# Two steps of the feed-forward weights' preparation, moved from the first full pass of a software pipeline into the second

## The reference, cut to what matters

```python
x = x + layernorm(attn(layernorm(x)))          # rotary on half of each head, softmax, Wo
# feed-forward, on xn = layernorm(x)
base   = xn @ W.T
proj   = l2norm(xn @ Wp.T + bp)                # 32 wide
logits = proj @ l2norm(sim) * exp(min(temp, CLAMP_MAX))
lw     = softmax(logits)                        # 4 experts, of ranks 1, 2, 4, 8
ret    = lw where the expert is the top one, else 0
res    = sum over experts of ret[e] * (xn @ Wd[e].T) @ Wu[e].T
x = x + layernorm(base + res)
```

## Time and profile before

| | us |
|---|---|
| median of 3 runs | 167.34 |
| the three runs | 165.85, 167.34, 168.54 |
| the profiled execution, own time | 168.68 |
| its span, first to last instruction | 166.9 |
| its mean granted TensorE clock | 0.92 |

### The profile page before, as it was taken

How to read it: one execution, slowest core, us unless ns; L and a number is a source line. 1 busy time by engine, 2 the same in 40 slices (tenths; PEclk the granted TensorE clock), 3 DMA queues, 4 the chain that set the end, 5 groups by cost and what they waited for, 6 DMA issues and landing times.

```text
span 166.9 us, 3027 instructions
## 1 busy us (share of the span) xinstructions
PE 132.7 (80%) x865; PEld 108.6 (65%) x865; DVE 131.6 (79%) x560; ACT 112.0 (67%) x369; POOL 90.6 (54%) x150
## 2 busy tenths in 40 slices
PE   0468589967998999999999999999999799256030
PEld 0246267855887869887977897797889589145020
DVE  4669947586888899899979998897898889774512
ACT  3167535955979699879969996997998667240130
POOL 6272850670465586849657774976469516405202
PEclk9999957999999999999999999999999999965555
DMA  4533240000000000100010010001001000101001
GB/s 106 174 83 108 68 121 0 6 0 0 2 0 4 2 0 0 67 0 0 2 67 2 0 41 22 4 0 63 2 6 63 0 4 13 50 0 63 2 0 63
DMA packets 4912, 5.02 MB, mean 30 GB/s; under 512 B 369, under 2 KB 4640, under 8 KB 4896
## 3 DMA queue, kind: packets, MB, share of 16 engines
q1 hardware_dynamic: 4512, 4.46, 8.5%
q10 hardware_dynamic: 384, 0.38, 1.0%
HBM read 2.74 MB, written 2.10 MB: 29 GB/s over the span
## 4 chain that ended last, share of the span: by engine, by line
PE 46%; DVE 23%; ACT 18%; POOL 4%; DMA 3%; issue 3%; POOLq 1%; DVEq 0%; ACTq 0%
PE ps_s L857 6%; PE ps_z L898 6%; PE ps_a L877 5%; ACT probs L321 5%; PE ps_b L831 4%; DVE neg_max L475 3%; DMA x_all<-x 3%; PE ps_c L877 3%; ACT sq_y L332 3%; PE ps_a L867 2%; DVE x_all L495 2%; PE ps_z L912 2%; ACT qk_t L316 2%; PE ps_b L877 2%; ACT sq_z L355 2%
## 5 line engine op out<-in xcount | busy, mean ns | idle before, releaser
L321 ACT ACTIVATE probs<-ps_s,neg_max 128x256 f32<-128x256 f32 x64 | 27.1, 486 | 11.8 <-DVE neg_max L475 11.8
L475 DVE TENSOR_REDUCE neg_max<-ps_s 128x2 f32<-128x512 f32 x32 | 21.6, 681 | 4.0 <-PE ps_s L857 4.0
L857 PE MATMUL ps_s<-qk_t 64*128 64x256 f32 x128 | 19.2, 418 | 0.9 <-ACT probs L321 0.9
L877 PE MATMUL ps_a<-v_all,probs_t 128*128 128x129 f32 x128 | 18.0, 283 | 0.0
L217 POOL TENSOR_TENSOR turn<-qk,sin_x 128x256 f32<-128x256 f32 x16 | 11.9, 746 | 9.7 <-ACT qk L305 9.3
L877 PEld LDWEIGHTS ps_a<-v_all,probs_t 128*128 128x128 f32 x128 | 15.6, 191 | 2.3 <-issue 2.3
L228 POOL TENSOR_TENSOR inv_norm<-norm,power 128x4 f32<-128x4 f32 x8 | 8.1, 1015 | 15.0 <-DVE norm L544 15.0
L898 PE MATMUL ps_z<-w_z,x_t 128*128 128x190 f32 x64 | 14.2, 357 | 2.0 <-DVE x_all L599 2.0
L857 PEld LDWEIGHTS ps_s<-qk_t 64*128 64x128 f32 x128 | 11.9, 195 | 5.8 <-issue 5.2
L232 POOL TENSOR_TENSOR rsy<-var_y,power 128x4 f32<-128x4 f32 x8 | 8.6, 1070 | 12.6 <-ACT sq_y L332 12.6
L495 DVE SCALAR_TENSOR_TENSOR x_all<-y_all,rsy,x_all 128x128 f32<-128x128 f32 x32 | 13.7, 448 | 0.8 <-POOL rsy L232 0.8
(11 more groups left out here) (205 smaller groups left out, 423.8 us busy)
## 6 DMA issues: line engine op xcount, KB each, us to landing
x_all<-x SPq DMA_DIRECT2D x8, 256.0 KB, 2.8
out<-x_all SPq DMA_DIRECT2D x7, 256.0 KB, 2.1
vec<-vectors ACTq DMA_DIRECT2D x1, 273.0 KB, 4.3
w_raw<-w_attn SPq DMA_DIRECT2D x1, 256.0 KB, 5.1
out<-x_all SPq DMA_DIRECT2D x2, 128.0 KB, 1.7
ffn_raw<-w_ffn ACTq DMA_DIRECT2D x1, 71.5 KB
down_raw<-w_down ACTq DMA_DIRECT2D x1, 23.5 KB
sim_raw<-sim ACTq DMA_DIRECT2D x1, 0.5 KB
```

Source lines behind the costliest of these rows:

```text
L321: last = act.activation(probs[:, u, j, :], ps_s[u % 2][:, j * T:(j + 1) * T], ACT.Exp, bias=neg_max[:, u, j:j + 1])
L475: dve.tensor_reduce(neg_max[:, u, :], ps_s[u % 2][:, :].rearrange("p (j k) -> p j k", j=TILES), AX.X, ALU.max, negate=True).then_inc(max_r ...
L857: last = pe.matmul(ps_s[h][:, j * T:(j + 1) * T], qk_t[r, b, 0, j * P:(j + 1) * P], qk_t[r, b, 1, :], start=True, stop=True)
L877: last = pe.matmul(unit_bank[u][:, j * VW:(j + 1) * VW], probs_t[:, u, i, j * P:(j + 1) * P], v_all[:, at:at + VW], start=(i == 0), stop=( ...
```

## The change

Four steps take another place. On DVE, part 2 moves from the middle of pass 0 to the place behind part 5 in pass 1; part 4 moves from the last place of pass 0 to the first of pass 1, which in DVE's order is the same place, since nothing stands between the two. On PE, part 2 moves from behind `weigh(0, 2)` to behind `scores(1, 0)`, so past `turn_x(2)` and the scores; part 3 moves behind the first two `project_qkv` of pass 1. The centred up weights now stay in columns 256 to 383 of `ps_z1`, because `ps_z0` is overwritten by the joint centring before they are read. The counts waited for change with the order. Every instruction keeps its shape and their number is the same; POOL, ACT and SP have the same programs.

```diff
@@ DVE, later_weights
-    last = dve.tensor_copy(wu_up[rr, t, :], ps_z0[rr, 0:E])
+    last = dve.tensor_copy(wu_up[rr, t, :], ps_z1[rr, 2 * P:2 * P + E])
...
-    last = dve.tensor_tensor(wu_low[rr, t, :], ps_z0[rr, 0:E], wu_up[rr, t, :].bitcast(F32), ALU.subtract)
+    last = dve.tensor_tensor(wu_low[rr, t, :], ps_z1[rr, 2 * P:2 * P + E], wu_up[rr, t, :].bitcast(F32), ALU.subtract)
@@ DVE, the loop
+    if a == 1:
+        later_weights(4)
     if done:
         add_bias(a - 2, 1)
     if nxt and a >= 0:
         rows_low(a + 1)
...
     if a == 1:
         later_weights(5)
+        later_weights(2)
...
         row_max(a, 3)
         weights_sum(a, 0)
-    if a == 0:
-        later_weights(2)
...
         add_head(a, 2, 1)
-    if a == 0:
-        later_weights(4)
@@ PE, later_weights
     elif part == 1:
         pe.wait_ge(post_dve, 2)
-        pe.matmul(ps_z0[:, 0:E], wu_raw..., centre[:, :],
+        pe.matmul(ps_z1[:, 2 * P:2 * P + E], wu_raw..., centre[:, :],
     elif part == 2:
-        pe.wait_ge(post_dve, 4)
+        pe.wait_ge(post_dve, 3)
...
     else:
-        pe.wait_ge(post_dve, 5)
+        pe.wait_ge(post_dve, 4)
@@ PE, the loop
-    if a == 1:
-        later_weights(3)
     if nxt:
         project_qkv(a + 1, 0, ...)
         project_qkv(a + 1, 1, ...)
+    if a == 1:
+        later_weights(3)
...
         weigh(a, 2)
-    if a == 0:
-        later_weights(2)
...
         scores(a + 1, 0, ...)
+    if a == 0:
+        later_weights(2)
     if now:
         weigh(a, 3)
```

More of the change, by code:

```diff
@@ L926, in later_weights @@
                     pe.wait_ge(post_dve, 2)
-                    pe.matmul(ps_z0[:, 0:E], wu_raw[:, :, :, :].rearrange("p t h c -> p (t h c)"), centre[:, :],
+                    pe.matmul(ps_z1[:, 2 * P:2 * P + E], wu_raw[:, :, :, :].rearrange("p t h c -> p (t h c)"), centre[:, :],
                               start=True, stop=True).then_inc(post_mm, 1)
                 elif part == 2:
-                    pe.wait_ge(post_dve, 4)
+                    pe.wait_ge(post_dve, 3)
                     pe.matmul(ps_z1[:, 0:RANK], down_raw[0:PROJ, :], sim_r[:, :], start=True, stop=True)
```

## The result

The changed kernel is slower: median 169.66 us of 20 runs against 168.19 us of 20 runs of the kernel before, ratio 1.0106 with a 95% interval of 1.0076 to 1.0137. The profiled execution took 170.04 us, its span is 168.2, 1.3 more than before, and its mean granted TensorE clock is 0.906 for 0.920.

What follows compares the result with a forecast made beforehand. Bound: the order of waits, no engine's sum. Terms -0.96, -0.31, +0.60, +2.43, -0.99, +0.8 and -0.95 gave +0.6, rounded to +0.5 on the median 167.34: 167.8 us, range 166.2 to 169.5.

Steps and rivals of the forecast that it cites:

- Part 4's wait behind the scores: End of pass 0: DVE waits in part 4 from about 37.7 to 39.37 for PE's products, now behind the scores.
- `row_max(1, 0)` about 1 us early: Entry of pass 1: of 2.19 us won on PE, 0.96 is left, so this maximum starts at 40.23 for 41.19.
- 2.4 us for part 2: Pass 1 on DVE: part 2's eight operations add 2.43 us ahead of `stats`, `residual_y(0, 0)` and `row_max(1, 2)`.
- one small statistic held by the third rope: Pass 1, behind `residual_y(0, 0)`: the five small statistics meet POOL's third rope operation, to 47.35, some 0.5 us lost.
- the two residual tiles free: Pass 1, behind `row_max(1, 2)`: the two tiles find POOL free and take 0.6 us for 1.55.
- `row_max(1, 3)` 0.55 late: Late in pass 1: this maximum at 49.15 for 48.60, so pass 2 is entered some 0.5 us late.
- +0.60 for the wait in part 5: Pass 1: the sum's term for DVE standing in part 5, some 0.5 us, until PE part 3 ends at 42.73.
- +0.8: Pass 1: first meetings with POOL, some 0.3 us lost on `residual_y(0, 0)` and 0.5 on the small statistics.
- -0.95: Pass 1: later meetings with POOL, time that comes back when the two residual tiles behind `row_max(1, 2)` find it free.
- rival 3: Late pass 1: PE without work 1.6 us, clock falls to half, 3.3 us late on top of 0.5: 171.1; chance 0.03.
- Rival 1: Pass 1: DVE is ahead of POOL's third rope or misses it, statistics cost nothing extra: 167.1 or 166.4; chance 0.27.
- rival 2: Pass 1: nothing comes back, residual tiles still meet POOL's later rope, `row_max(1, 3)` 1.5 late: 168.8; chance 0.15.

Runs made afterwards that it cites:

- e8: The changed kernel plus 3 extra PE products in the second idle time alone, ahead of `turn_x2`; ratio 1.0001 to the kernel before.
- e11: e5 made late on purpose: 12 unread statistics (2.4 us) on DVE behind part 5 in pass 1; ratio 1.0024 to the kernel before.
- e1: The changed kernel plus 8 extra unread PE products, 5 and 3, in its two PE idle times; ratio 0.9971 to the kernel before.
- e12: e11 plus 5 and 3 extra unread PE products in the two PE idle times; ratio 1.0007 to the kernel before.
- e3: The kernel before with only PE parts 2 and 3 moved, DVE part 2 staying in pass 0; ratio 0.9935 to the kernel before.
- e5: The changed kernel with DVE part 2 back in pass 0, in two halves where DVE stood idle; ratio 0.9857 to the kernel before.
- e6: e5 with DVE part 4 moved behind `row_max(1, 0)`; ratio 0.9855 to the kernel before.
- e10: e5 with PE parts 2 and 3 at their old places; ratio 0.9870 to the kernel before.
- e4: The changed kernel with DVE part 2 split: four roundings stay in pass 0, four remainders go to pass 1; ratio 0.9941 to before.

## Why the prediction was wrong

- **The order, step by step: right.** Part 4's wait behind the scores, `row_max(1, 0)` about 1 us early (1.0 against the second pair of maxima, forecast 0.96), the wait of 0.39 in part 5 (forecast 0.5), 2.4 us for part 2, one small statistic held by the third rope, the two residual tiles free. I had `row_max(1, 3)` 0.55 late; measured against the same start it is 0.23. Of the 0.3 between, 0.07 had come by `row_max(1, 1)`, 0.12 lie in the term "+0.60 for the wait in part 5" (against `row_max(1, 1)` its copy is 0.48 later), and 0.1 in the meetings with POOL: the tile lost 0.21 and the statistic 0.54, so 0.75 for the +0.8, and 1.02 came back for the -0.95.
- **The step that failed** is rival 3, "PE's clock falls", with its chance of 0.03, and in it the sentence "Against: near the end PE idles 2 us and is still granted full clock". I had its mechanism and its place, the late `row_max(1, 2)`, and I had written down an idle time of 1.6 us for PE (it was 1.36); I left out the second one, 0.82 ahead of `turn_x2`, without which e8 shows no fall. In its place the runs show a fall in 16 of 20 executions, worth 1.25 us. It was the earlier trace rows that misled: an idle stretch at full clock says nothing of what is granted behind it. PE stood idle there for 4.24 us, from 142.74 to 146.98. Two more rows of the kernel before, PE by stretches at the end of that idle time, would have shown it:

```profile
146.50:147.00 0.50, 0.02 (x1) 0.98 0.00 0
147.00:147.50 0.50, 0.35 (x1) 0.50 0.00 0
```

  There the lower clock comes as PE takes up work again. In the changed kernel it comes at 51.2, half a microsecond behind the end of the second idle time; in e11 at about 49.4, just inside it. e1 and e12 take both idle times away, e8 the second alone, and the fall is gone with them; e11 brings it back without the moved work.
- **Its price** was 3.3 us, for half speed as long as at the start of the run. It lasted some 3.4 us instead of 6.5, and it cost 1.25 (B). From the transposes behind `turn_x2` to `project_z` PE took 3.35 us in the changed kernel and 1.77 in e1, so 1.58 more. Of these 0.27 came back ahead of `turn_x`, for whose rows PE in e1 waits on ACT.
- **Rival 1** (the gain kept) and **rival 2** (nothing comes back) didn't occur in the changed kernel, but each has its run: e3 and e5 show one of the two tiles getting past the rope, e6 and e10 show both meeting it again.
- **The baseline** is nearly half of the miss of 1.86 us (169.66 against 167.8): 167.34 was drawn 0.85 below the median of 20. The change's own 1.47 us (169.66 - 168.19) is close to the 0.23 of A and the 1.25 of B, because the median execution is one with the fall. That it fits so well is in part luck: with the fall in 16 of 20, A and B make 1.23 us on average, and the means are 1.36 apart.
- That no later pass changes its length was right: in the chain of the changed kernel the first maxima of passes 2, 3 and 4 begin at 57.75, 72.88 and 87.99, so 15.13 and 15.11 apart.

## What to carry to other kernels

Moving work off a visible wait paid here where the place it landed in had idle time of its own (e5, 1.4% faster); sent into the next pass, half of it paid 0.6% (e4) and the whole lost 1%. So read the idle times of the profile after the move, and put the work there. When a change makes PE stand idle twice close behind each other, as here for 1.36 and 0.82 us with one group of transposes between, count a fall of the clock as a likely case, priced from a stretch of the same trace at half clock. Where DVE's and GpSimd's operations on SBUF meet, a shift of 0.3 us decided here whether 0.45 us more were lost, so small gains ahead of such a place need not arrive.

## What the runs showed of the hardware that I had not expected

- With idle times of 1.36 and 0.82 us and 0.66 us of transposes between, TensorE's granted clock fell to 1.2 GHz for about 3.4 us in 16 of 20 executions (0.95 and 0.83 us: 4 of 12; 0.55 and 0.82: 0 of 12; 1.36 alone, the second filled: 0 of 6). It began at 51.2, behind the second idle time, in the changed kernel, and at 49.4, just ahead of its end, in e11.
- Extra matmuls whose results nobody reads made the kernel faster, by 1.25 us of B.
- VectorE's `scalar_tensor_tensor` of two SBUF tensors is held by GpSimd's operations of 128x256 (0.82 to 0.90 us for 0.35), but not by its power of 128x4 (0.35 beside a power of 1.01 us).
